# Unused bytes between the operand blocks of a matmul stream on one Trainium2 core

## The chip, the cores and the metric

The kernel runs on one core of one Trainium2 chip. The metric is the device time of one execution in microseconds (us); the lower the better. Three runs of the kernel before are given, and one execution of it was profiled. Engines are named as in the profile: PE is TensorE (matmuls), PEld its weight loads, DVE is VectorE, ACT is ScalarE, POOL is GpSimd and SP is SyncE, which issues the DMAs.

## The reference, cut to what matters

The input x is 16 sequences of 128 x 128. A mixture of experts with all eight experts evaluated densely, and a shared expert, are added to it, and then a 128 x 128 matrix picked for each sequence is applied and added.

```python
# x (16,128,128), gating (16,8), sg (16,1,1); Wg, Wu (8,128,512), Wd (8,512,128)
g = einsum('bsd,edf->ebsf', x, Wg);  u = einsum('bsd,edf->ebsf', x, Wu)
expert_outs = einsum('ebsf,efd->ebsd', silu(g) * u, Wd)
expert_output = einsum('be,ebsd->bsd', gating, expert_outs)
shared = einsum('bsf,fd->bsd', silu(x @ Sg) * (x @ Su), Sd)
x = x + (1 - sg) * expert_output + sg * shared
out = x + einsum('bij,bjk->bik', T[step - 1], x)
```

## The kernel before, in words

Everything is held transposed: features on the 128 partitions, and the 16 x 128 = 2048 tokens in the free dimension, in NT = 4 tiles of W = 512 columns. The hidden dimension of 512 is cut into NC = 4 chunks of 128. An expert is thus 16 units (4 tiles x 4 chunks), and with the shared expert there are 9 x 16 = 144 units.

To keep accuracy at the speed of the type fp32r, each fp32 operand is split into a high part (the value rounded to fp32r, `_hi`) and a low part (the rest, `_lo`), and each product is three matmuls: high x high, high x low and low x high. A unit n has three products and so nine matmuls of 512 columns, each with its own weight load of 128 columns:

- `project_g` (lines 444 to 446, into `g_bank`) multiplies gate weights by the x tile,
- `project_u` (the same lines, into `u_bank`) the up weights by the x tile,
- `project_down` (lines 470, 471 and 473, into `o_bank`) the down weights by the h tile of two units before (LAG = 2).

144 units are 1296 such matmuls. Between them ACT computes silu (L278), DVE multiplies (L342), ACT rounds h into `h_hi` (L284), DVE subtracts to get `h_lo` (L348). Every four units DVE scales the expert's output (L356) and POOL adds it to `acc` (L260).

The weights arrive by DMA in `w_raw`, which holds two experts (slots), four chunks and three matrices. For every expert POOL rounds each chunk of three blocks at once into `w_hi` (L217, 128 x 384) and subtracts for `w_lo` (L212); the first expert's are rounded by ACT (L297) and subtracted by DVE (L382) and POOL (L212), in other shapes. The x tiles are split once, in the beginning (L294, L307, L233, L385). The order of the PE work is the program's: no scheduler is involved. Semaphores guard each hand-over, and PE waits for a new expert's weights at the first unit of an expert.

Tiles lie in SBUF one behind the other in the order of their declaration. A weight block is 128 x 4 bytes = 512 bytes on each partition, an x tile or h tile 2048 bytes, and each tensor declared ahead of them has a multiple of 512 bytes.

The end of the program transposes the result (L483), multiplies by the picked matrices (L491) and stores.

Of the kernel before, what the change touches and what calls it, by code (L numbers as in the profile page):

```python
# [5 lines left out]
P = 128  # L6
# [6 lines left out]
def moe_then_step_kernel(  # L13
# [33 lines left out]
    W = BT * S  # L47
# [6 lines left out]
    PEEL_DVE = 5  # L54
    EARLY = 3
    Q = 32
    assert NC == 4 and NT == 4 and E % 2 == 0

    with ExitStack() as ctx:
# [6 lines left out]
        x_nat = sb("x_nat", [P, BT, D])  # L66
        x_blk = sb("x_blk", [P, B, S])
        zero = sb("zero", [P, P])
        x_hi = sb("x_hi", [P, NT, W], F32R)
        x_lo = sb("x_lo", [P, NT, W], F32R)  # L70
        w_raw = sb("w_raw", [P, 2, NC, 3, P])
        w_hi = sb("w_hi", [P, 2, NC, 3, P], F32R)
        w_lo = sb("w_lo", [P, 2, NC, 3, P], F32R)
        silu_g = sb("silu_g", [P, 2, W])
        h_hi = sb("h_hi", [P, HR, W], F32R)
        h_lo = sb("h_lo", [P, HR, W], F32R)
        scaled = sb("scaled", [P, 2, W])
        acc = sb("acc", [P, NT, W])
        yT = sb("yT", [P, NT, W])
# [123 lines left out]
        @block.gpsimd  # L203
        def _(pool):
            nc.gpsimd.memset(ident[:, :], 0.0).then_inc(ident_done, 1)
            pool.wait_ge(ident_done, 1)
            nc.gpsimd.affine_select(out=ident[:, :], in_=ident[:, :], compare_op=ALU.not_equal, fill=1.0, base=0,
                                    pattern=[[-1, P]], channel_multiplier=1).then_inc(ident_done, 1)

            def low_part(slot, c, m):  # L210

                return nc.gpsimd.tensor_tensor(w_lo[:, slot, c, m, :], w_raw[:, slot, c, m, :],  # L212
                                               w_hi[:, slot, c, m, :].bitcast(F32), ALU.subtract)

            def split_chunk(slot, c, count):

                nc.gpsimd.tensor_copy(w_hi[:, slot, c, :, :], w_raw[:, slot, c, :, :]).then_inc(w_rounded, 1)  # L217
                pool.wait_ge(w_rounded, count + 1)
                low_part(slot, c, slice(0, 3)).then_inc(w_ready, 1)


            pool.wait_ge(w0_rounded, 3)
            low_part(0, 1, slice(0, 2)).then_inc(w_ready, 1)
            pool.wait_ge(w0_rounded, 4)
            low_part(0, 2, slice(0, 2)).then_inc(w_ready, 1)
            low_part(0, 3, slice(0, 2)).then_inc(w_ready, 1)
            pool.wait_ge(w0_rounded, 5)
            low_part(0, slice(0, NC), 2).then_inc(w_ready, 1)

            def split_x(t):  # L230

                pool.wait_ge(x_rounded, t + 1)
                nc.gpsimd.tensor_tensor(x_lo[:, t, :], acc[:, t, :], x_hi[:, t, :].bitcast(F32),  # L233
                                        ALU.subtract).then_inc(acc_done, 1)

            split_x(1)

            pool.wait_ge(c_in, 32)
            nc.gpsimd.tensor_scalar(rest_b[:, :], share_b[:, :], -1.0, 1.0, ALU.mult, ALU.add).then_inc(coef_step, 1)
            nc.gpsimd.tensor_copy(coef[:, E * B:(E + 1) * B], share_b[:, :]).then_inc(coef_step, 1)  # L240
            pool.wait_ge(coef_step, 2)
            nc.gpsimd.tensor_tensor(coef[:, 0:E * B].rearrange("p (e b) -> p b e", b=B), route_b[:, :, :],
                                    rest_b[:, :].unsqueeze(2).to_broadcast([P, B, E]), ALU.mult).then_inc(coef_step, 1)
            for t in range(2, NT):
                split_x(t)

            with pool.Fori(0, E, 2) as e:
                for par in range(2):  # L250
                    slot = (par + 1) % 2
                    for t in range(NT):
                        group = NT * (e + par) + t
                        if t == 0:

                            pool.wait_ge(w_in[slot], 24 * e + 48)

                        pool.wait_ge(acc_done, group + NT - 1)
                        pool.wait_ge(scaled_done, group + 1)
                        nc.gpsimd.tensor_tensor(acc[:, t, :], acc[:, t, :], scaled[:, t % 2, :], ALU.add).then_inc(acc_done, 1)  # L260
                        if t < 2:
                            for c in (2 * t, 2 * t + 1):
                                split_chunk(slot, c, NC * (e + par) + c)


            for t in range(NT):
                tile = slice(t * BT, (t + 1) * BT)
                pool.wait_ge(T_turned, t + 1)
                nc.gpsimd.tensor_tensor(T_plus[:, tile, :], T_turn[:, tile, :],
                                        ident[:, :].unsqueeze(1).to_broadcast([P, BT, P]), ALU.add).then_inc(T_done, 1)  # L270

        @block.scalar
        def _(act):
# [6 lines left out]
            def round_h(n, k):  # L280


                act.wait_ge(h_done, n + 1)
                nc.scalar.activation(h_hi[:, k % HR, :], u_bank[k % HR][:, :], ACT.Copy).then_inc(h_rounded, 1)  # L284

            def copy_y(i):
                b, nb = parts[i]
# [3 lines left out]

            def round_x(t):
                act.wait_ge(x_turned, t)
                nc.scalar.activation(x_hi[:, t, :], acc[:, t, :], ACT.Copy).then_inc(x_rounded, 1)  # L294

            def round_w0(c, m):
                nc.scalar.activation(w_hi[:, 0, c, m, :], w_raw[:, 0, c, m, :], ACT.Copy).then_inc(w0_rounded, 1)  # L297


            act.wait_ge(zero_done, 1)  # L300
# [3 lines left out]
            act.wait_ge(wu0_in, 16)  # L304
            round_w0(0, 1)
            act.wait_ge(x0_turned, 1)
            nc.scalar.activation(x_hi[:, 0, :], o_bank[0][:, :], ACT.Copy).then_inc(x_rounded, 1)  # L307
            act.wait_ge(w0_in, 32)
            round_w0(1, slice(0, 2))
            round_w0(slice(2, NC), slice(0, 2))  # L310
# [26 lines left out]
        def _(dve):  # L337
# [7 lines left out]
            def split_h(n, k):  # L345

                dve.wait_ge(h_rounded, n + 1)
                nc.vector.tensor_tensor(h_lo[:, k % HR, :], u_bank[k % HR][:, :], h_hi[:, k % HR, :].bitcast(F32),  # L348
                                        ALU.subtract).then_inc(split_done, 1)

            def scale_group(m0, t):
# [27 lines left out]
            for m in range(2):  # L379

                dve.wait_ge(w0_rounded, m + 1)
                nc.vector.tensor_tensor(w_lo[:, 0, 0, m, :], w_raw[:, 0, 0, m, :], w_hi[:, 0, 0, m, :].bitcast(F32),  # L382
                                        ALU.subtract).then_inc(split_done, 1)
            dve.wait_ge(x_rounded, 1)
            nc.vector.tensor_tensor(x_lo[:, 0, :], o_bank[0][:, :], x_hi[:, 0, :].bitcast(F32),  # L385
                                    ALU.subtract).then_inc(split_done, 1)

            nc.vector.tensor_copy(acc[:, 0, :], o_bank[0][:, :])
# [52 lines left out]
        def _(pe):  # L441
            def product(bank, w, x_h, x_l, start, stop):

                nc.tensor.matmul(bank, w_hi[:, w[0], w[1], w[2], :], x_h, start=start, stop=False)  # L444
                nc.tensor.matmul(bank, w_hi[:, w[0], w[1], w[2], :], x_l, start=False, stop=False)  # L445
                return nc.tensor.matmul(bank, w_lo[:, w[0], w[1], w[2], :], x_h, start=False, stop=stop)  # L446

            def project_g(n, k):

                t, c = k % U // NC, k % NC  # L450

                pe.wait_ge(g_read, n - 1)
                product(g_bank[k % 2][:, :], (k // U % 2, c, 0), x_hi[:, t, :], x_lo[:, t, :],
                        True, True).then_inc(g_done, 1)

            def project_u(n, k):
                t, c = k % U // NC, k % NC
                if k >= LAG:

                    pe.wait_ge(split_done, EARLY + n + 1 - HR)  # L460
                product(u_bank[k % HR][:, :], (k // U % 2, c, 1), x_hi[:, t, :], x_lo[:, t, :],
                        True, True).then_inc(u_done, 1)

            def project_down(n, k):
# [2 lines left out]
                w = (k // U % 2, c, 2)  # L467

                pe.wait_ge(h_rounded, n + 1)
                nc.tensor.matmul(o_bank[t % 2][:, :], w_hi[:, w[0], w[1], w[2], :], h_hi[:, slot, :], start=c == 0, stop=False)  # L470
                nc.tensor.matmul(o_bank[t % 2][:, :], w_lo[:, w[0], w[1], w[2], :], h_hi[:, slot, :], start=False, stop=False)  # L471
                pe.wait_ge(split_done, EARLY + n + 1)
                last = nc.tensor.matmul(o_bank[t % 2][:, :], w_hi[:, w[0], w[1], w[2], :], h_lo[:, slot, :],  # L473
                                        start=False, stop=c == NC - 1)
                if c == NC - 1:
                    last.then_inc(o_done, 1)
# [30 lines left out]
            warm_up(2)  # L507

            pe.wait_ge(x_rounded, 1)
            nc.tensor.matmul(g_bank[0][:, :], w_hi[:, 0, 0, 0, :], x_hi[:, 0, :], start=True, stop=False)  # L510
            pe.wait_ge(split_done, 1)
            nc.tensor.matmul(g_bank[0][:, :], w_lo[:, 0, 0, 0, :], x_hi[:, 0, :], start=False, stop=False)
            pe.wait_ge(split_done, EARLY)
            nc.tensor.matmul(g_bank[0][:, :], w_hi[:, 0, 0, 0, :], x_lo[:, 0, :], start=False, stop=True).then_inc(g_done, 1)
            project_u(0, 0)

            pe.wait_ge(w_ready, 1)
            product(g_bank[1][:, :], (0, 1, 0), x_hi[:, 0, :], x_lo[:, 0, :], True, True).then_inc(g_done, 1)
            project_u(1, 1)
            with pe.Fori(0, N_ROUTED // U, 2) as e:  # L520
                for k in range(LAG, 2 * U + LAG):
# [56 lines left out]
```

## Time and profile before

| | |
|---|---|
| median of 3 runs | 312.31 us (312.09 to 312.71) |
| the profiled execution | 312.09 us |
| its span, first to last instruction | 310.1 us |
| busy shares of the span | PE 99%, PEld 82%, DVE 70%, ACT 53%, POOL 33% |
| share of PE in the chain that ended last | 95% |
| granted TensorE clock | full speed (2.4 GHz) in all slices |

A matmul's record is longer than the time to the start of the next one, since they are pipelined; the busy share of PE therefore says less than the distance between starts.

### The profile page before, as it was taken

To read this page: it belongs to the slowest core of one execution; us is meant where nothing else is said; L and a number is where in the kernel's file an instruction comes from. 1 tells how busy PE (TensorE), PEld (TensorE's weight loads), DVE (VectorE), ACT (ScalarE), POOL (GpSimd) and SP (SyncE) were. 2 spreads that over 40 slices of the span, in tenths; PEclk is the share of its full clock that TensorE was granted. 3 is DMA by queue.
4 is the path that set the end of the run, shared out by engine and by line. 5 is a ranking of instruction groups with operands and counts; after the bars stand their busy time and mean duration, and the time that the engine had idled before them with its cause. 6 is when DMAs were issued, how large, how long until landed. Compare 5 with 4: busy or idle time off the path is not lost.

```text
span 310.1 us, 4762 instructions
## 1 busy us (share of the span) xinstructions
PE 305.5 (99%) x1364; PEld 253.3 (82%) x1364; DVE 217.5 (70%) x355; ACT 164.6 (53%) x306; POOL 102.2 (33%) x116
## 2 busy tenths in 40 slices
PE   8999999999999999999999999999999999999996
PEld 7688888888888888888888888888888888888885
DVE  2786667766676666776667766677666766668885
ACT  5565555555555555555555555555555555555552
POOL 2565312441155115511552134411441155111310
PEclk9999999999999999999999999999999999999999
DMA  6930300030001100030003001100013000000112
GB/s 159 201 89 2 103 1 2 0 94 7 1 0 45 56 0 0 0 101 0 0 0 109 13 13 17 17 14 13 15 17 110 0 0 0 0 2 0 34 36 68
DMA packets 32727, 10.39 MB, mean 34 GB/s; under 512 B 16208, under 2 KB 32720, under 8 KB 32720
## 3 DMA queue, kind: packets, MB, share of 16 engines
q1 hardware_dynamic: 32720, 10.30, 13.5%
q8 instruction: 4, 0.07, 0.1%
q14 instruction: 3, 0.02, 0.0%
HBM read 9.25 MB, written 1.05 MB: 33 GB/s over the span
## 4 chain that ended last, share of the span: by engine, by line
PE 95%; SPq 1%; DMA 1%; POOL 0%; DVE 0%; ACT 0%; issue 0%
PE o_bank L470 11%; PE o_bank L473 11%; PE o_bank L471 11%; PE g_bank L446 10%; PE u_bank L446 10%; PE g_bank L445 10%; PE u_bank L445 10%; PE g_bank L444 10%; PE u_bank L444 10%; DMA w_raw<-in_L_cond_Wd 1%; PE o_bank L491 1%; SPq L158 1%; PE o_bank L483 0%; POOL w_lo L212 0%; DVE res L371 0%; PE u_bank L483 0%
## 5 line engine op out<-in xcount | busy, mean ns | idle before, releaser
L342 DVE TENSOR_TENSOR u_bank<-u_bank,silu_g 128x512 f32<-128x512 f32 x144 | 100.7, 699 | 84.2 <-PE u_bank L446 82.6
L278 ACT ACTIVATE silu_g<-g_bank 128x512 f32<-128x512 f32 x144 | 86.1, 598 | 132.8 <-PE g_bank L446 132.4
L348 DVE TENSOR_TENSOR h_lo<-u_bank,h_hi 128x512 fp32r<-128x512 f32 x144 | 97.9, 680 | 0.1
L260 POOL TENSOR_TENSOR acc<-acc,scaled 128x512 f32<-128x512 f32 x32 | 41.5, 1296 | 163.2 <-DVE scaled L356 163.0
L284 ACT ACTIVATE h_hi<-u_bank 128x512 fp32r<-128x512 f32 x144 | 85.4, 593 | 0.7 <-DVE u_bank L342 0.7
L470 PE MATMUL o_bank<-h_hi,w_hi 128*128 128x512 f32 x144 | 56.2, 390 | 0.8 <-POOL w_lo L212 0.8
L444 PE MATMUL u_bank<-x_hi,w_hi 128*128 128x512 f32 x144 | 56.1, 390 | 0.0
L473 PE MATMUL o_bank<-h_lo,w_hi 128*128 128x512 f32 x144 | 56.0, 389 | 0.0
L445 PE MATMUL u_bank<-x_lo,w_hi 128*128 128x512 f32 x144 | 56.0, 389 | 0.0
L471 PE MATMUL o_bank<-h_hi,w_lo 128*128 128x512 f32 x144 | 56.0, 389 | 0.0
L446 PE MATMUL u_bank<-x_hi,w_lo 128*128 128x512 f32 x144 | 56.0, 389 | 0.0
L444 PE MATMUL g_bank<-x_hi,w_hi 128*128 128x512 f32 x143 | 56.0, 392 | 0.0
L445 PE MATMUL g_bank<-x_lo,w_hi 128*128 128x512 f32 x143 | 55.7, 389 | 0.0
L446 PE MATMUL g_bank<-x_hi,w_lo 128*128 128x512 f32 x143 | 55.6, 389 | 0.0
L212 POOL TENSOR_TENSOR w_lo<-w_raw,w_hi 128x384 fp32r<-128x384 f32 (+2 forms) x36 | 35.8, 998 | 9.1 <-ACT w_hi L297 6.5
L470 PEld LDWEIGHTS o_bank<-h_hi,w_hi 128*128 128x128 f32 x144 | 27.0, 188 | 6.7 <-POOL w_lo L212 1.2
L445 PEld LDWEIGHTS u_bank<-x_lo,w_hi 128*128 128x128 f32 x144 | 27.1, 188 | 5.7
L444 PEld LDWEIGHTS u_bank<-x_hi,w_hi 128*128 128x128 f32 x144 | 27.2, 189 | 5.6
L473 PEld LDWEIGHTS o_bank<-h_lo,w_hi 128*128 128x128 f32 x144 | 27.0, 188 | 5.7 <-DVE h_lo L348 0.2
L471 PEld LDWEIGHTS o_bank<-h_hi,w_lo 128*128 128x128 f32 x144 | 27.0, 188 | 5.6
L446 PEld LDWEIGHTS u_bank<-x_hi,w_lo 128*128 128x128 f32 x144 | 27.0, 188 | 5.6
L446 PEld LDWEIGHTS g_bank<-x_hi,w_lo 128*128 128x128 f32 x143 | 26.8, 188 | 5.5
(49 smaller groups left out, 151.2 us busy)
## 6 DMA issues: line engine op xcount, KB each, us to landing
w_raw<-in_L_cond_Wd SPq DMA_DIRECT2D x8, 256.0 KB, 3.9
w_raw<-in_L_cond_Wg SPq DMA_DIRECT2D x7, 256.0 KB, 3.1
w_raw<-in_L_cond_Wu SPq DMA_DIRECT2D x7, 256.0 KB, 3.8
T_blk<-in_L_cond_T SPq DMA_DIRECT2D x64, 16.0 KB, 1.6
out_y<-res SPq DMA_DIRECT2D x3, 256.0 KB, 2.3
x_blk<-in_x SPq DMA_DIRECT2D x4, 128.0 KB, 3.6
x_nat<-in_x SPq DMA_DIRECT2D x1, 256.0 KB, 2.8
x_blk<-in_x SPq DMA_DIRECT2D x4, 64.0 KB, 2.7
```

Source lines behind the costliest of these rows:

```text
L212: return nc.gpsimd.tensor_tensor(w_lo[:, slot, c, m, :], w_raw[:, slot, c, m, :], w_hi[:, slot, c, m, :].bitcast(F32), ALU.subtract)
L260: nc.gpsimd.tensor_tensor(acc[:, t, :], acc[:, t, :], scaled[:, t % 2, :], ALU.add).then_inc(acc_done, 1)
L278: nc.scalar.activation(silu_g[:, k % 2, :], g_bank[k % 2][:, :], ACT.Silu).then_inc(g_read, 1)
L284: nc.scalar.activation(h_hi[:, k % HR, :], u_bank[k % HR][:, :], ACT.Copy).then_inc(h_rounded, 1)
L342: nc.vector.tensor_tensor(u_bank[k % HR][:, :], u_bank[k % HR][:, :], silu_g[:, k % 2, :], ALU.mult).then_inc(h_done, 1)
L348: nc.vector.tensor_tensor(h_lo[:, k % HR, :], u_bank[k % HR][:, :], h_hi[:, k % HR, :].bitcast(F32), ALU.subtract).then_inc(split_done, 1)
L444: nc.tensor.matmul(bank, w_hi[:, w[0], w[1], w[2], :], x_h, start=start, stop=False)
L445: nc.tensor.matmul(bank, w_hi[:, w[0], w[1], w[2], :], x_l, start=False, stop=False)
L446: return nc.tensor.matmul(bank, w_lo[:, w[0], w[1], w[2], :], x_h, start=False, stop=stop)
L470: nc.tensor.matmul(o_bank[t % 2][:, :], w_hi[:, w[0], w[1], w[2], :], h_hi[:, slot, :], start=c == 0, stop=False)
L471: nc.tensor.matmul(o_bank[t % 2][:, :], w_lo[:, w[0], w[1], w[2], :], h_hi[:, slot, :], start=False, stop=False)
L473: last = nc.tensor.matmul(o_bank[t % 2][:, :], w_hi[:, w[0], w[1], w[2], :], h_lo[:, slot, :], start=False, stop=c == NC - 1)
```

## The change

The tensors get unused columns of 4 bytes: each weight block in `w_hi` and `w_lo` is followed by 4 (16 bytes, so blocks are 528 bytes apart and no longer 512), each x tile in `x_hi` and `x_lo` by 16 (64 bytes, 2112 in place of 2048), and each h tile in `h_hi` and `h_lo` by 8 (32 bytes, 2080 in place of 2048). All accesses name the used columns. `w_raw`, `acc` and all others keep their shapes, but lie elsewhere, as the tensors ahead of them have grown. No instruction is added, removed or moved. Wherever an instruction writes or reads several blocks of `w_hi` or `w_lo` at once, its access is no longer one run but one run for each block.

```diff
+    WP = P + 4
+    XP = W + 16
+    HP = W + 8
...
-        x_hi = sb("x_hi", [P, NT, W], F32R)
-        x_lo = sb("x_lo", [P, NT, W], F32R)
+        x_hi = sb("x_hi", [P, NT, XP], F32R)
+        x_lo = sb("x_lo", [P, NT, XP], F32R)
         w_raw = sb("w_raw", [P, 2, NC, 3, P])
-        w_hi = sb("w_hi", [P, 2, NC, 3, P], F32R)
-        w_lo = sb("w_lo", [P, 2, NC, 3, P], F32R)
+        w_hi = sb("w_hi", [P, 2, NC, 3, WP], F32R)
+        w_lo = sb("w_lo", [P, 2, NC, 3, WP], F32R)
         silu_g = sb("silu_g", [P, 2, W])
-        h_hi = sb("h_hi", [P, HR, W], F32R)
-        h_lo = sb("h_lo", [P, HR, W], F32R)
+        h_hi = sb("h_hi", [P, HR, HP], F32R)
+        h_lo = sb("h_lo", [P, HR, HP], F32R)
...
-                nc.gpsimd.tensor_copy(w_hi[:, slot, c, :, :], w_raw[:, slot, c, :, :]).then_inc(w_rounded, 1)
+                nc.gpsimd.tensor_copy(w_hi[:, slot, c, :, 0:P], w_raw[:, slot, c, :, :]).then_inc(w_rounded, 1)
...
-                nc.scalar.activation(h_hi[:, k % HR, :], u_bank[k % HR][:, :], ACT.Copy).then_inc(h_rounded, 1)
+                nc.scalar.activation(h_hi[:, k % HR, 0:W], u_bank[k % HR][:, :], ACT.Copy).then_inc(h_rounded, 1)
...
-                nc.tensor.matmul(bank, w_hi[:, w[0], w[1], w[2], :], x_h, start=start, stop=False)
-                nc.tensor.matmul(bank, w_hi[:, w[0], w[1], w[2], :], x_l, start=False, stop=False)
-                return nc.tensor.matmul(bank, w_lo[:, w[0], w[1], w[2], :], x_h, start=False, stop=stop)
+                nc.tensor.matmul(bank, w_hi[:, w[0], w[1], w[2], 0:P], x_h, start=start, stop=False)
+                nc.tensor.matmul(bank, w_hi[:, w[0], w[1], w[2], 0:P], x_l, start=False, stop=False)
+                return nc.tensor.matmul(bank, w_lo[:, w[0], w[1], w[2], 0:P], x_h, start=False, stop=stop)
```

The other changed lines put `0:P` or `0:W` in place of `:` in the same way.

## Rows read from the trace of the kernel before

**Rows 1.** The page's chain that ended last, by engine.

```profile
PE 95%; SPq 1%; DMA 1%; POOL 0%; DVE 0%; ACT 0%; issue 0%
```

**Rows 2.** The chain in order of time: start us, us, what.

```profile
11.45 0.50 PE o_bank L470
...
302.86 0.44 PE o_bank L483 x4
...
304.69 0.89 PE o_bank L491 x8
305.58 0.66 PE u_bank L483 x4
```

**Rows 3.** Waits of PE: engine line, waited for, us, times, longest.

```profile
PE o_bank L470 <- POOL w_lo L212: 0.8, 1, 0.8
```

**Rows 4.** Timeline of one unit: start us, us, engine, line, operation.

```profile
102.05 0.39 PE L444 MATMUL g_bank<-x_hi,w_hi 128*128 128x512 f32 x1
102.05 0.19 PEld L445 LDWEIGHTS g_bank<-x_lo,w_hi 128*128 128x128 f32 x1
...
102.27 0.39 PE L445 MATMUL g_bank<-x_lo,w_hi 128*128 128x512 f32 x1
...
102.73 0.39 PE L444 MATMUL u_bank<-x_hi,w_hi 128*128 128x512 f32 x1
...
103.41 0.39 PE L470 MATMUL o_bank<-h_hi,w_hi 128*128 128x512 f32 x1
...
104.09 0.39 PE L444 MATMUL g_bank<-x_hi,w_hi 128*128 128x512 f32 x1
```

**Rows 5.** PE in windows as long as an expert: busy us (records), clock, DMA.

```profile
20.00:52.64 32.64, 32.64 (x146) 1.00 0.09 26
...
150.56:183.20 32.64, 32.64 (x146) 1.00 0.13 32
...
248.48:281.12 32.64, 32.64 (x146) 1.00 0.00 1
```

**Rows 6.** Tile w_hi: duration ns min/median/max, first and last start us.

```profile
L444 PE MATMUL u_bank<-x_hi,w_hi x144: 389/389/465, 7.0 to 300.7; 128*128 128x512 f32 x144
...
L470 PEld LDWEIGHTS o_bank<-h_hi,w_hi x144: 186/188/190, 11.4 to 303.6; 128*128 128x128 f32 x144
L470 PE MATMUL o_bank<-h_hi,w_hi x144: 389/389/497, 11.4 to 303.8; 128*128 128x512 f32 x144
```

**Rows 7.** Timeline: the unit after the first wait for weights.

```profile
12.02 0.39 PE L473 MATMUL o_bank<-h_lo,w_hi 128*128 128x512 f32 x1
...
14.10 0.39 PE L473 MATMUL o_bank<-h_lo,w_hi 128*128 128x512 f32 x1
```

**Rows 8.** POOL's groups by form: busy us, mean ns, idle before.

```profile
L212 POOL TENSOR_TENSOR w_lo<-w_raw,w_hi 128x384 fp32r<-128x384 f32 x32 | 32.4, 1014 | 2.6
L217 POOL CAST w_hi<-w_raw 128x384 fp32r<-128x384 f32 x32 | 16.2, 507 | 0.0
...
L212 POOL TENSOR_TENSOR w_lo<-w_raw,w_hi 128x256 fp32r<-128x256 f32 x3 | 2.1, 736 | 5.1 <-ACT w_hi L297 5.1
L212 POOL TENSOR_TENSOR w_lo<-w_raw,w_hi 128x512 fp32r<-128x512 f32 x1 | 1.3, 1277 | 1.4 <-ACT w_hi L297 1.4
```

**Rows 9.** POOL's timeline around the weights of one expert.

```profile
93.47 1.29 POOL L260 TENSOR_TENSOR acc<-acc,scaled 128x512 f32<-128x512 f32 x1 [3.85 <-DVE scaled L356]
...
96.84 1.02 POOL L212 TENSOR_TENSOR w_lo<-w_raw,w_hi 128x384 fp32r<-128x384 f32 x1
101.63 1.29 POOL L260 TENSOR_TENSOR acc<-acc,scaled 128x512 f32<-128x512 f32 x1 [3.77 <-DVE scaled L356]
```

**Rows 10.** ACT's groups by form.

```profile
L284 ACT ACTIVATE h_hi<-u_bank 128x512 fp32r<-128x512 f32 x144 | 85.4, 593 | 0.7 <-DVE u_bank L342 0.7
...
L297 ACT ACTIVATE w_hi<-w_raw 128x512 fp32r<-128x512 f32 x2 | 1.2, 624 | 1.5 <-DMA w_raw<-in_L_cond_Wd 1.5
```

More of the change, by code:

```diff
@@ L210, in low_part @@
             def low_part(slot, c, m):
-                return nc.gpsimd.tensor_tensor(w_lo[:, slot, c, m, :], w_raw[:, slot, c, m, :],
-                                               w_hi[:, slot, c, m, :].bitcast(F32), ALU.subtract)
+                return nc.gpsimd.tensor_tensor(w_lo[:, slot, c, m, 0:P], w_raw[:, slot, c, m, :],
+                                               w_hi[:, slot, c, m, 0:P].bitcast(F32), ALU.subtract)
             def split_chunk(slot, c, count):
-                nc.gpsimd.tensor_copy(w_hi[:, slot, c, :, :], w_raw[:, slot, c, :, :]).then_inc(w_rounded, 1)
+                nc.gpsimd.tensor_copy(w_hi[:, slot, c, :, 0:P], w_raw[:, slot, c, :, :]).then_inc(w_rounded, 1)
                 pool.wait_ge(w_rounded, count + 1)
@@ L232, in split_x @@
                 pool.wait_ge(x_rounded, t + 1)
-                nc.gpsimd.tensor_tensor(x_lo[:, t, :], acc[:, t, :], x_hi[:, t, :].bitcast(F32),
+                nc.gpsimd.tensor_tensor(x_lo[:, t, 0:W], acc[:, t, :], x_hi[:, t, 0:W].bitcast(F32),
                                         ALU.subtract).then_inc(acc_done, 1)
@@ L293, in round_x @@
                 act.wait_ge(x_turned, t)
-                nc.scalar.activation(x_hi[:, t, :], acc[:, t, :], ACT.Copy).then_inc(x_rounded, 1)
+                nc.scalar.activation(x_hi[:, t, 0:W], acc[:, t, :], ACT.Copy).then_inc(x_rounded, 1)
             def round_w0(c, m):
-                nc.scalar.activation(w_hi[:, 0, c, m, :], w_raw[:, 0, c, m, :], ACT.Copy).then_inc(w0_rounded, 1)
+                nc.scalar.activation(w_hi[:, 0, c, m, 0:P], w_raw[:, 0, c, m, :], ACT.Copy).then_inc(w0_rounded, 1)
             act.wait_ge(zero_done, 1)
@@ L306, in _ @@
             act.wait_ge(x0_turned, 1)
-            nc.scalar.activation(x_hi[:, 0, :], o_bank[0][:, :], ACT.Copy).then_inc(x_rounded, 1)
+            nc.scalar.activation(x_hi[:, 0, 0:W], o_bank[0][:, :], ACT.Copy).then_inc(x_rounded, 1)
             act.wait_ge(w0_in, 32)
@@ L347, in split_h @@
                 dve.wait_ge(h_rounded, n + 1)
-                nc.vector.tensor_tensor(h_lo[:, k % HR, :], u_bank[k % HR][:, :], h_hi[:, k % HR, :].bitcast(F32),
+                nc.vector.tensor_tensor(h_lo[:, k % HR, 0:W], u_bank[k % HR][:, :], h_hi[:, k % HR, 0:W].bitcast(F32),
                                         ALU.subtract).then_inc(split_done, 1)
@@ L381, in _ @@
                 dve.wait_ge(w0_rounded, m + 1)
-                nc.vector.tensor_tensor(w_lo[:, 0, 0, m, :], w_raw[:, 0, 0, m, :], w_hi[:, 0, 0, m, :].bitcast(F32),
+                nc.vector.tensor_tensor(w_lo[:, 0, 0, m, 0:P], w_raw[:, 0, 0, m, :], w_hi[:, 0, 0, m, 0:P].bitcast(F32),
                                         ALU.subtract).then_inc(split_done, 1)
             dve.wait_ge(x_rounded, 1)
-            nc.vector.tensor_tensor(x_lo[:, 0, :], o_bank[0][:, :], x_hi[:, 0, :].bitcast(F32),
+            nc.vector.tensor_tensor(x_lo[:, 0, 0:W], o_bank[0][:, :], x_hi[:, 0, 0:W].bitcast(F32),
                                     ALU.subtract).then_inc(split_done, 1)
@@ L452, in project_g @@
                 pe.wait_ge(g_read, n - 1)
-                product(g_bank[k % 2][:, :], (k // U % 2, c, 0), x_hi[:, t, :], x_lo[:, t, :],
+                product(g_bank[k % 2][:, :], (k // U % 2, c, 0), x_hi[:, t, 0:W], x_lo[:, t, 0:W],
                         True, True).then_inc(g_done, 1)
@@ L460, in project_u @@
                     pe.wait_ge(split_done, EARLY + n + 1 - HR)
-                product(u_bank[k % HR][:, :], (k // U % 2, c, 1), x_hi[:, t, :], x_lo[:, t, :],
+                product(u_bank[k % HR][:, :], (k // U % 2, c, 1), x_hi[:, t, 0:W], x_lo[:, t, 0:W],
                         True, True).then_inc(u_done, 1)
@@ L469, in project_down @@
                 pe.wait_ge(h_rounded, n + 1)
-                nc.tensor.matmul(o_bank[t % 2][:, :], w_hi[:, w[0], w[1], w[2], :], h_hi[:, slot, :], start=c == 0, stop=False)
-                nc.tensor.matmul(o_bank[t % 2][:, :], w_lo[:, w[0], w[1], w[2], :], h_hi[:, slot, :], start=False, stop=False)
+                nc.tensor.matmul(o_bank[t % 2][:, :], w_hi[:, w[0], w[1], w[2], 0:P], h_hi[:, slot, 0:W], start=c == 0, stop=False)
+                nc.tensor.matmul(o_bank[t % 2][:, :], w_lo[:, w[0], w[1], w[2], 0:P], h_hi[:, slot, 0:W], start=False, stop=False)
                 pe.wait_ge(split_done, EARLY + n + 1)
-                last = nc.tensor.matmul(o_bank[t % 2][:, :], w_hi[:, w[0], w[1], w[2], :], h_lo[:, slot, :],
+                last = nc.tensor.matmul(o_bank[t % 2][:, :], w_hi[:, w[0], w[1], w[2], 0:P], h_lo[:, slot, 0:W],
                                         start=False, stop=c == NC - 1)
@@ L509, in _ @@
             pe.wait_ge(x_rounded, 1)
-            nc.tensor.matmul(g_bank[0][:, :], w_hi[:, 0, 0, 0, :], x_hi[:, 0, :], start=True, stop=False)
+            nc.tensor.matmul(g_bank[0][:, :], w_hi[:, 0, 0, 0, 0:P], x_hi[:, 0, 0:W], start=True, stop=False)
             pe.wait_ge(split_done, 1)
-            nc.tensor.matmul(g_bank[0][:, :], w_lo[:, 0, 0, 0, :], x_hi[:, 0, :], start=False, stop=False)
+            nc.tensor.matmul(g_bank[0][:, :], w_lo[:, 0, 0, 0, 0:P], x_hi[:, 0, 0:W], start=False, stop=False)
             pe.wait_ge(split_done, EARLY)
-            nc.tensor.matmul(g_bank[0][:, :], w_hi[:, 0, 0, 0, :], x_lo[:, 0, :], start=False, stop=True).then_inc(g_done, 1)
+            nc.tensor.matmul(g_bank[0][:, :], w_hi[:, 0, 0, 0, 0:P], x_lo[:, 0, 0:W], start=False, stop=True).then_inc(g_done, 1)
             project_u(0, 0)
             pe.wait_ge(w_ready, 1)
-            product(g_bank[1][:, :], (0, 1, 0), x_hi[:, 0, :], x_lo[:, 0, :], True, True).then_inc(g_done, 1)
+            product(g_bank[1][:, :], (0, 1, 0), x_hi[:, 0, 0:W], x_lo[:, 0, 0:W], True, True).then_inc(g_done, 1)
             project_u(1, 1)
```

## The prediction

> **What bounds the kernel now.** I read the page's chain first: 95% of the span lies on PE [rows 1]. The chain in order of time shows where PE's stream begins and ends: it starts in earnest at 11.45 us and hands over to the tail of small transposes and matmuls at 305.58 us [rows 2]. The view of PE's waits has one wait of this stream, 0.8 us for the first expert's low weights at 11.45 us [rows 3]; after it PE waits for nobody. So the time is a number of matmuls by the distance between their starts, and the third view is the timeline of one unit. From the start of its first matmul at 102.05 us to that of the next unit's at 104.09 us pass 2.04 us for nine matmuls, 226.7 ns each [rows 4]. The windows of an expert's length confirm it to the last digit: a stretch of 32.64 us holds 16 units, and each of them has the same 146 records (144 matmuls and the two cut by its edges) at full clock [rows 5]; there are eight such windows from 20 to 281 us, of which three stand there.
>
> The sum: before 11.45 us PE has done the g and u products of units 0, 1 and 2, 18 matmuls. The other 1278 by 226.7 ns are 289.7 us. Three transposes of 0.44 us and three steps of 0.89 us between them are 4.0 us [rows 2]. From 305.58 us to the end of the span are 4.5 us. 11.45 + 289.7 + 4.0 + 4.5 = 309.7 us, against a span of 310.1 us; the 0.4 us left are units a little slower right after an interruption, as the one from 12.02 to 14.10 us, 2.08 us in place of 2.04 [rows 7]. The profiled execution took 312.09 us, 2.0 us more than its span, and lies 0.2 us under the median of 312.31 us.
>
> At 2.4 GHz, 226.7 ns are 544 cycles for 512 columns. 32 cycles (13.3 ns) are thus not columns, 17.3 us over 1296 matmuls, and whether the change reaches them is the whole question.
>
> **The change part by part.**
>
> *PE's two reads.* While the 512 columns of one matmul are read, the weights of the next are loaded: the load of L445 starts at 102.05 us with the matmul of L444, and its record is 0.19 us long [rows 4]. Do these two reads hinder each other by where they lie? Before, all weight blocks begin at multiples of 512 bytes and all tiles too, so the pairs differ in their distance, but never in the distance modulo 512 bytes. What the trace excludes: a hindrance that depends on the address above 512 bytes. A window of an expert's length runs through 4 x tiles, 4 h slots and 12 blocks of high and of low weights, the windows alternate between both weight slots, and the pairs lie from next to each other to tens of kilobytes apart. Yet g, u and down products are alike spaced [rows 4], all windows hold the same count [rows 5], and weight loads vary only from 186 to 190 ns over 144 records [rows 6]. What the trace can't exclude is a hindrance by the low nine bits of the address, since those are now the same for all.
>
> Two things speak against this as well. First, the two reads go at different paces: the load's 128 columns of 4 bytes in at most 188 ns and the matmul's 512 in some 213 ns, so while the load reads its 512 bytes the matmul reads some 1.8 KB, and the one passes the other's place modulo 512 more than twice. A constant offset of 16 to 500 bytes between the starts shifts when they meet, not how often. Second, other readers and writers of SBUF come and go (DMA at a share of 0.13 and of 0.00 [rows 5], POOL reading and writing weights at one time and idle at another [rows 9]) at any address, and the 226.7 ns don't move. I take 0 ns per matmul. Bounds: the most that can be won is all of the 13.3 ns, 17.3 us; the most that can be lost, by the nearest row in which the stream went slower (2.08 us a unit, 4.4 ns per matmul [rows 7]), is 5.8 us. The value is near neither end: no row shows a dependence on address at all. The smallest step of a synchronous stream, one cycle of 0.42 ns in each matmul, would be 0.54 us.
>
> A rule of the Trainium skill speaks against a gain here: the page "TensorE: Matmul & The Clock Gate", section "Step-by-step: what each phase is for", says that the engine has two independent SBUF read ports, one for the moving operand and one for the weight load, which takes no bandwidth from the running matmul. By it the sum stays at 312.3 us; the trace agrees as far as the spacing doesn't vary with the pair, and can't show what the spacing would be without a load.
>
> *POOL's splits.* The cast L217 writes three runs of 128 in place of one of 384, and L212 reads and writes such. It may cost nothing: L212 took 1277 ns in the form of 4 blocks that already lie apart (the third matrix of all chunks) and 1014 and 736 ns in the joined forms of 3 and 2 blocks; the steps are 278 and 263 ns per block, so lying apart shows no cost [rows 8]. If both got a third dearer, a pair of chunks would take 4.1 us in place of 3.0 us. Its cover: after L212 at 96.84 us POOL idles 3.8 us until the next sum at 101.63 us [rows 9], and the weights split there by 97.86 us are needed only at the next expert's first unit, which is the one at 104.09 us [rows 4] (the sum at 101.63 us is that of the third tile, which DVE scales just ahead of the fifteenth unit): 6.2 us of slack. Without that cover each expert would pay 2 us. I take 0.
>
> *ACT and DVE.* `h_hi` and `h_lo` are still one run of 512 each; ACT's 593 ns [rows 10] and DVE's have no cause to change, and PE doesn't wait for either [rows 3]. The first expert's rounding by ACT is on the path: the wait of 0.8 us at 11.45 us hangs behind L297 of the down weights and L212 of 1277 ns. Both already step over blocks (every third one), so only the step changes, from 1536 to 1584 bytes. 0 us; at worst L212 pays the rate of its dearest form (736 ns for 256, or 2.88 ns for each element, against 2.49), 0.2 us, and ACT the difference of 624 to 593 ns, 0.03 us [rows 8, 10].
>
> *Everything else.* Tensors behind lie at other addresses, still multiples of 128 bytes as the padded sizes add up; DMAs have the same pieces and PE waits for none. 0 us.
>
> Sum: 0 us on the profiled execution's 312.09 us, and on the median: 312.3 us.
>
> **The rivals.**
>
> *A: the 32 cycles are a conflict of equal low addresses, and spreading them dissolves it.* For it: 32 is also the number of 16-byte pieces in a weight block's row of 512 bytes, and today every pair has the same phase. Against it: the differing paces. All gone gives 312.3 - 17.3 = 295.0 us; half of it, if the new phases still meet in half of the pairs, 303.7 us. The same page of the Trainium skill (section "Back-to-back issue gap") gives N / 2.4 + 2.5 ns between warm matmuls. By that rule 10.8 ns of the spacing here would be avoidable and the time an estimated 298.3 us; no run here shows 215.8 ns.
>
> *B, the other side: blocks that start off a round address are read more slowly.* Today all start at multiples of 512 bytes. After it, of the 24 weight blocks of a tensor no two would begin at the same place modulo 512, half begin off 32 bytes, and every second h tile off 64 bytes. A weight load has cover: 188 ns in a spacing of 226.7 ns, so it must grow by more than 38 ns to be seen. A moving read has none, each ns shows. If the odd h slots alone pay the 4.4 ns of the slow unit [rows 7], 216 matmuls make 1.0 us: 313.3 us. If all pay, 5.8 us: 318.1 us. It decides from 0.5 ns a matmul on average. The same price holds where equal phases are free of conflict today and the new ones are not.
>
> *C: POOL gets so slow with broken runs that weights come late.* A pair of chunks takes 3.0 us and has 6.2 us until PE needs it [rows 4, 9]; it would have to triple. I give it no price but a place in "slower".
>
> **How the numbers follow.** Differences within 0.2% (0.6 us) can't be told from none; the three runs before span that much. No effect: 0.80. Rival A: 0.09, all of it faster. Rival B and C: 0.11, slower. The forecast is that of the likeliest, 312.3 us. The range takes one cycle a matmul either way (0.54 us), the spread of the runs (0.2 below, 0.4 above) and the 0.2 us of the start above: 311.5 to 313.4, and leaves out rival A and the dear half of B. That is some 15 in 100.
>
> **What the profile of the changed kernel would show.** Right: units of 2.04 us, the same 146 records in 32.64 us, loads of 188 ns, matmul records of 389 ns, L217 near 507 and L212 near 1014 ns, the first wait near 0.8 us. Rival A: fewer than 2.04 us a unit, and units that differ from each other, as the pairs now differ in phase. Rival B: moving reads of h (L470, L471, L473) spaced wider than those of x, in every second unit. C: PE waits for w_lo of L212 beyond the first. The prediction is wrong if the spacing depends on the low bits of an address, which no pair of the kernel before could show.

## The result, and the profile after

The changed kernel takes 317.91 us (median of 3 runs, 317.58 to 317.91) against 312.31 us: a ratio of 1.0174, with an interval of 1.0151 to 1.0197. It is 5.6 us slower, where 312.3 us was forecast with a range up to 313.4 us. The profiled execution has a span of 315.8 us, 5.7 us more than before.

The page's chain by engine reads as before [rows 1]: PE holds the end, and nobody else has moved into the chain.

```profile
PE 95%; SPq 1%; DMA 1%; POOL 0%; DVE 0%; ACT 0%; issue 0%
```

The chain in order of time (start us, us, what) answers to [rows 2]. PE's stream of down products begins 0.55 us earlier, since the first down weights happened to land sooner, and it ends 5.66 us later. All of the loss, and 0.55 us more, lies within the stream.

```profile
10.90 0.49 PE o_bank L473
...
308.53 0.44 PE o_bank L486 x4
310.35 0.89 PE o_bank L494 x8
311.24 0.66 PE u_bank L486 x4
```

PE's waits have no new row (L473 is L470 of before, the lines are three further down); the one that answers to [rows 3] is a little shorter:

```profile
PE o_bank L473 <- POOL w_lo L215: 0.6, 1, 0.6
```

The same windows of an expert's length as in [rows 5] (busy us, records, clock, DMA share, GB/s) hold 142 or 143 records and no longer 146, at the same clock:

```profile
20.00:52.64 32.64, 32.64 (x142) 1.00 0.09 26
...
85.28:117.92 32.64, 32.64 (x143) 1.00 0.08 24
```

So the matmuls are further apart, all along the stream. One window of 260 us, from 20 to 280 us, measures it: before it held 1149 records, after 1124. Less the two that the edges cut, the mean distance between starts was 260 / 1147 = 226.7 ns and is 260 / 1122 = 231.7 ns. Over the 1278 matmuls of the stream these 5.0 ns are 6.4 us; less the 0.55 us of earlier start that is 5.8 us, against the 5.7 us by which the span grew.

```profile
20.00:280.00 260.00, 260.00 (x1124) 1.00 0.09 22
```

The timeline of PE shows two things that answer to [rows 4]: a unit now takes 2.08 us (101.33 to 103.41), and the steps within it are no longer alike, some 0.22 or 0.23 us and some 0.24 us.

```profile
101.33 0.39 PE L447 MATMUL g_bank<-x_hi,w_hi 128*128 128x512 f32 x1
101.56 0.40 PE L448 MATMUL g_bank<-x_lo,w_hi 128*128 128x512 f32 x1
101.80 0.39 PE L449 MATMUL g_bank<-x_hi,w_lo 128*128 128x512 f32 x1
102.03 0.39 PE L447 MATMUL u_bank<-x_hi,w_hi 128*128 128x512 f32 x1
102.25 0.39 PE L448 MATMUL u_bank<-x_lo,w_hi 128*128 128x512 f32 x1
102.48 0.39 PE L449 MATMUL u_bank<-x_hi,w_lo 128*128 128x512 f32 x1
102.71 0.39 PE L473 MATMUL o_bank<-h_hi,w_hi 128*128 128x512 f32 x1
102.94 0.40 PE L474 MATMUL o_bank<-h_hi,w_lo 128*128 128x512 f32 x1
103.18 0.39 PE L476 MATMUL o_bank<-h_lo,w_hi 128*128 128x512 f32 x1
103.41 0.39 PE L447 MATMUL g_bank<-x_hi,w_hi 128*128 128x512 f32 x1
```

The pattern belongs to the pairs and not to chance: two experts (66.7 us) later, at the same blocks and tiles, the same steps come back, 0.24 us behind L448 among them.

```profile
168.05 0.39 PE L447 MATMUL g_bank<-x_hi,w_hi 128*128 128x512 f32 x1
168.28 0.40 PE L448 MATMUL g_bank<-x_lo,w_hi 128*128 128x512 f32 x1
168.52 0.39 PE L449 MATMUL g_bank<-x_hi,w_lo 128*128 128x512 f32 x1
```

The records of the single instructions say little on where it lies: in the view of tile w_hi (duration ns min/median/max, first and last start us; compare [rows 6]) the weight load still takes 188 ns, while the matmul's record grew from 389 to 394 ns. A matmul's end is modelled, so its 5 ns are a hint only, and that the load's record stays as it was holds for this kernel and not for all (see w_shift below).

```profile
L473 PEld LDWEIGHTS o_bank<-h_hi,w_hi x144: 186/188/190, 10.9 to 309.3; 128*128 128x128 f32 x144
L473 PE MATMUL o_bank<-h_hi,w_hi x144: 387/394/494, 10.9 to 309.5; 128*128 128x512 f32 x144
```

And POOL's groups by form cost what they did [rows 8], broken runs or not:

```profile
L215 POOL TENSOR_TENSOR w_lo<-w_raw,w_hi 128x384 fp32r<-128x384 f32 x32 | 32.6, 1019 | 2.6
L220 POOL CAST w_hi<-w_raw 128x384 fp32r<-128x384 f32 x32 | 16.2, 507 | 0.0
```

### The profile page after: what moved, and what is told of

It is laid out like the page before. It is cut to its first block, busy times and chain, and to the rows that moved or that the text cites. A ratio compares the mean times of both kernels' runs of the same rounds, so it can differ in the third digit from the quotient of the medians.

```text
span 315.8 us, 4762 instructions
## 1 busy us (share of the span) xinstructions
PE 311.3 (99%) x1364; PEld 252.8 (80%) x1364; DVE 217.8 (69%) x355; ACT 164.8 (52%) x306; POOL 102.4 (32%) x116
## 4 chain that ended last, share of the span: by engine, by line
PE 95%; SPq 1%; DMA 1%; POOL 0%; DVE 0%; ACT 0%; issue 0%
PE o_bank L473 11%; PE o_bank L474 11%; PE o_bank L476 11%; PE u_bank L447 10%; PE u_bank L449 10%; PE u_bank L448 10%; PE g_bank L447 10%; PE g_bank L448 10%; PE g_bank L449 10%; DMA w_raw<-in_L_cond_Wd 1%; PE o_bank L494 1%; SPq L161 1%; PE o_bank L486 0%; POOL w_lo L215 0%; DVE res L374 0%; PE u_bank L486 0%
## 5 line engine op out<-in xcount | busy, mean ns | idle before, releaser
L473 PE MATMUL o_bank<-h_hi,w_hi 128*128 128x512 f32 x144 | 57.0, 396 | 0.6 <-POOL w_lo L215 0.6
L474 PE MATMUL o_bank<-h_hi,w_lo 128*128 128x512 f32 x144 | 56.8, 394 | 0.0
L449 PE MATMUL u_bank<-x_hi,w_lo 128*128 128x512 f32 x144 | 56.7, 394 | 0.0
L476 PE MATMUL o_bank<-h_lo,w_hi 128*128 128x512 f32 x144 | 56.7, 394 | 0.0
L448 PE MATMUL u_bank<-x_lo,w_hi 128*128 128x512 f32 x144 | 56.7, 394 | 0.0
L448 PE MATMUL g_bank<-x_lo,w_hi 128*128 128x512 f32 x143 | 56.2, 393 | 0.0
L473 PEld LDWEIGHTS o_bank<-h_hi,w_hi 128*128 128x128 f32 x144 | 27.0, 188 | 7.2 <-POOL w_lo L215 1.0
L448 PEld LDWEIGHTS u_bank<-x_lo,w_hi 128*128 128x128 f32 x144 | 27.0, 188 | 6.2
L447 PEld LDWEIGHTS g_bank<-x_hi,w_hi 128*128 128x128 f32 x143 | 26.9, 188 | 6.2 <-POOL w_lo L215 0.2
```

The lines of the kernel that those rows point to most:

```text
L447: nc.tensor.matmul(bank, w_hi[:, w[0], w[1], w[2], 0:P], x_h, start=start, stop=False)
L448: nc.tensor.matmul(bank, w_hi[:, w[0], w[1], w[2], 0:P], x_l, start=False, stop=False)
L449: return nc.tensor.matmul(bank, w_lo[:, w[0], w[1], w[2], 0:P], x_h, start=False, stop=stop)
```

## The experiments

Each kernel ran beside the kernel before on the same chip; its ratio is against that. The kernel before took 311.5 to 311.8 us there. The spacing is the mean distance between starts, worked out as above from the records in the window from 20 to 280 us of the one execution that was profiled; the time and the ratio are of all executions.

Where blocks and tiles lie: all starts of the kernel before are equal modulo 512 bytes. They are not multiples of 512, as the text ahead of the result has it, but lie 128 bytes past one; only their differences are multiples. "Distance" below is the start of the weight blocks less the start of the tiles, modulo 256, and is 0 for it.

**One pad at a time.** The edits set two of the three pads back to nothing:

```diff
-    WP, XP, HP = P + 4, W + 16, W + 8    # the change
+    WP, XP, HP = P + 4, W, W             # w_pads
+    WP, XP, HP = P, W + 16, W            # x_pads
+    WP, XP, HP = P, W, W + 8             # h_pads
```

Expected, of w_pads, x_pads and h_pads in this order:

> Only the weight blocks are padded (528 bytes apart), the x and h tiles lie as before. Theory 1, the distance modulo 512 bytes between the weight block being loaded and the tile being read sets the cost, so that any spread of the phases costs the whole amount: about 317.5 to 318 us, 231.5 ns per matmul on average, for x and h products alike. Theory 2, the start of the weight block off a multiple of 32 or 64 bytes costs: the same 317.5 to 318 us. Theory 3, the start of the moving tile costs: 312.3 us, 226.7 ns.

> Only the x tiles are padded (2112 bytes apart). Theory 1 (distance modulo 512): the distance is 64, 128 or 192 bytes off today's for three of four tiles and 256 off for the low part, so the 864 gate and up matmuls pay for most of their pairs and the 432 down matmuls pay nothing: 312.3 + about 700 x 4.9 ns = 315.7 us. Theory 2 (start of the weight block): 312.3 us. Theory 3 (start of the moving tile): 312.3 us where 64 bytes are round enough, otherwise as theory 1.

> Only the h tiles are padded (2080 bytes apart). Theory 1 (distance modulo 512): three of four h slots are off today's distance, so about 324 of the 432 down matmuls pay 4.9 ns, 313.9 us, and the gate and up matmuls keep 226.7 ns. Theory 2: 312.3 us. Theory 3: 313.4 to 313.9 us.

Measured: w_pads 318.24 us (ratio 1.0204, interval 1.0187 to 1.0221), 231.7 ns; x_pads 316.88 us (1.017, 1.0153 to 1.0187), 230.7 ns; h_pads 315.02 us (1.01, 1.0083 to 1.0117), 229.3 ns; the window held 1124, 1129 and 1136 records. Each pad costs by itself, the weights' at least as much as all three. Theories 2 and 3 fall as the only cause, since the x and h pads cost with all weight blocks on starts equal modulo 512 as before, and the weights' pads cost with all tiles so. The pads don't add up (6.5, 5.1 and 3.2 us against 5.6 us together), as one has to expect if what counts is whether a pair is off, and not by how many pads. The theory's numbers miss: x_pads and h_pads were to cost 3.4 and 1.6 us. In part it is the count and the price that were off. By the addresses 648 pairs of x_pads are off, and 360 of h_pads in place of the 324 expected, since the padding moves the whole tensor `h_lo` by 128 bytes. At the 6.7 ns that a wrong distance of 16 or 32 bytes costs below, these would be 4.3 and 2.4 us. The rest falls on matmuls whose own pairs are at 0: in x_pads these are 229.1 ns from the next on average, not 226.7, and in h_pads the x products, all at 0, are 227.7 ns. The timeline of x_pads shows how:

```profile
79.37 0.39 PE L473 MATMUL o_bank<-h_hi,w_hi 128*128 128x512 f32 x1
79.60 0.39 PE L474 MATMUL o_bank<-h_hi,w_lo 128*128 128x512 f32 x1
79.83 0.39 PE L476 MATMUL o_bank<-h_lo,w_hi 128*128 128x512 f32 x1
80.05 0.40 PE L447 MATMUL g_bank<-x_hi,w_hi 128*128 128x512 f32 x1
...
83.54 0.40 PE L473 MATMUL o_bank<-h_hi,w_hi 128*128 128x512 f32 x1
83.78 0.39 PE L474 MATMUL o_bank<-h_hi,w_lo 128*128 128x512 f32 x1
84.01 0.39 PE L476 MATMUL o_bank<-h_lo,w_hi 128*128 128x512 f32 x1
84.24 0.40 PE L447 MATMUL g_bank<-x_hi,w_hi 128*128 128x512 f32 x1
```

At 79.37 us the first x tile is in use, whose distances are 0 here too, and three down products take 0.68 us. At 83.54 us it is the next tile, 64 bytes off, and the three down products take 0.70 us, though their own distances are still 0. In all units of the window whose x tile is the first the three take 0.680 us, in all whose x tile is the second 0.697 or 0.698 us. A matmul's loss thus reaches over to its neighbours.

**The same distance for all pairs.** With no pads, only the place of the weights was moved (and for `all_shift` that of x, h and weights together), by asking for a longer run and using it from an offset:

```diff
-        w_hi = sb("w_hi", [P, 2, NC, 3, P], F32R)
+        w_hi = sb("w_hi", [P, 2 * NC * 3 * P + 128], F32R)[:, 4:4 + 2 * NC * 3 * P].rearrange(
+            "p (a b c d) -> p a b c d", a=2, b=NC, c=3, d=P)     # 4 columns = 16 bytes
```

The offset was 4 in w_shift, 8, 16, 32 and 64 in w_shift32, 64, 128 and 256, and 124, 120 and 96 in w_back16, 32 and 128; the all_shift kernels do it for all six tensors, xh_shift16 for those of x and h alone.

Expected, of w_shift, w_shift32, w_shift64, w_shift128, w_back128, w_shift256, w_back16 and w_back32 in this order:

> No pads between blocks, but all weight blocks of both tensors begin 16 bytes later, so that every pair of block and tile has the same distance modulo 512, 16 bytes more than before. Theory 1: all 1296 matmuls are spaced alike again, at a value other than 226.7 ns if a distance of 16 bytes matters (about 231 ns, 318 us), and at 226.7 ns if that distance is one of the free ones. Theory 2 (a block that begins off 32 bytes costs): all spaced alike and wider, by about twice 4.9 ns if only the half of the blocks that lie off 32 bytes paid in the changed kernel: 318 to 325 us. Theory 4, only a variety of phases costs, as when the reads fall into step with each other in a uniform stream: 312.3 us.

> Weight blocks alone begin 32 bytes later; every pair has the distance 32 modulo 512. Distance theory: one uniform spacing again, above 226.7 ns unless 32 is a free distance; I expect 230 to 236 ns and 316 to 323 us. Start theory (off 32 bytes costs): back at 312 us, since the blocks begin at a multiple of 32 bytes again.

> Weight blocks alone begin 64 bytes later, starts on multiples of 32, distance 64 for all. If every distance off a multiple of 256 costs: 231 to 233.5 ns, 318 to 320.5 us. If the period were 64: 311.8 us; but 128 bytes already cost 5.7 ns, so that would be odd.

> Weight blocks alone begin 128 bytes later. In the kernel with padded x tiles the pairs at 128 or 384 bytes modulo 512 had mixed spacings and those at 256 kept 226.7 ns. Distance theory with a period of 256 bytes: a cost, 229 to 234 ns, 315 to 321 us. Distance theory with a period of 128 or less: 312 us. Start theory: 312 us.

> Weight blocks begin 384 bytes later: 128 bytes short of the old phase, which is also 128 ahead if the period is 256. Period 256: the same as 128 bytes ahead, 232.4 ns, 318.8 us. Period 512: another value, as behind is cheaper than ahead: 226.7 to 229 ns.

> Weight blocks alone begin 256 bytes later. In the kernel with padded x tiles the pairs at a distance of 256 bytes modulo 512 kept 226.7 ns. Distance theory with a period of 256 bytes: 311.5 us, 226.7 ns everywhere. Period of 512: 229 to 234 ns, 315 to 321 us.

> Weight blocks alone begin 496 bytes later, 16 bytes short of the old phase. If only the size of the distance counts, the same as 16 bytes ahead: 233.3 ns, 320.3 us. If the order counts (which of the two reads comes to a place first, since they run at different paces), another value; it may even lie under 226.7 ns, and then a version faster than the kernel before exists.

> Weight blocks begin 480 bytes later, 32 bytes short of the old phase, on a multiple of 32. 16 bytes short cost 1.7 ns, 16 ahead 6.7, 32 ahead 6.7. If a distance behind is cheap as such: 226.7 to 229 ns, 311.5 to 314.5 us. If the cost grows with the distance either way: 233 ns, 320 us.

| kernel | distance | us | ratio (interval) | spacing |
|---|---|---|---|---|
| w_shift | +16 | 320.29 | 1.0276 (1.0259 to 1.0293) | 233.4 ns |
| w_shift32 | +32 | 319.96 | 1.0275 (1.0257 to 1.0292) | 233.4 ns |
| w_shift64 | +64 | 319.94 | 1.0264 (1.0246 to 1.0283) | 233.6 ns |
| w_shift128 | +128 | 318.76 | 1.0246 (1.0224 to 1.0267) | 232.6 ns |
| w_back128 | -128 | 318.78 | 1.0222 (1.0205 to 1.0239) | 232.6 ns |
| w_back32 | -32 | 320.26 | 1.0264 (1.0242 to 1.0285) | 233.4 ns |
| w_back16 | -16 | 313.52 | 1.0056 (1.0037 to 1.0075) | 228.3 ns |
| w_shift256 | 256 = 0 | 311.89 | 0.9996 (0.9986 to 1.0006) | 226.7 ns |

Four windows, of w_shift, w_back16, w_shift128 and w_shift256 in this order, with the counts from which the spacings come:

```profile
20.00:280.00 260.00, 260.00 (x1116) 1.00 0.09 22
```

```profile
20.00:280.00 260.00, 260.00 (x1141) 1.00 0.09 22
```

```profile
20.00:280.00 260.00, 260.00 (x1120) 1.00 0.09 22
```

```profile
20.00:280.00 260.00, 260.00 (x1149) 1.00 0.09 22
```

What follows: no variety is needed, one wrong distance for all costs more (7 to 8.5 us) than the change's mixture, except 16 bytes behind (2.1 us). The period is 256 bytes: 256 is free, and 128 ahead and 128 behind have the same spacing (and 7.3 and 7.0 us over the kernel before on their chips). The idea that a distance behind is cheap as such was wrong (32 behind costs all of it), and so was the hope for a distance better than 0. Why 16 bytes behind costs only 1.7 ns, I can't say. A distance of 16 either way always has a start off 32 bytes in it, so these two rows don't show the distance alone; the other six do.

"Uniform" is the distance and not the step. In w_shift the steps are 230 to 236 ns, but in w_shift128, where the distance is the same for all pairs, they go from 228 to 241 ns and come back every seven matmuls, while the program's unit is nine long. At 10 ns the timeline shows it in the matmuls' records, three of 0.40 us and four of 0.39 us:

```profile
101.39 0.40 PE L476 MATMUL o_bank<-h_lo,w_hi 128*128 128x512 f32 x1
101.62 0.40 PE L447 MATMUL g_bank<-x_hi,w_hi 128*128 128x512 f32 x1
101.86 0.40 PE L448 MATMUL g_bank<-x_lo,w_hi 128*128 128x512 f32 x1
102.09 0.39 PE L449 MATMUL g_bank<-x_hi,w_lo 128*128 128x512 f32 x1
102.32 0.39 PE L447 MATMUL u_bank<-x_hi,w_hi 128*128 128x512 f32 x1
102.56 0.39 PE L448 MATMUL u_bank<-x_lo,w_hi 128*128 128x512 f32 x1
102.78 0.39 PE L449 MATMUL u_bank<-x_hi,w_lo 128*128 128x512 f32 x1
103.01 0.40 PE L473 MATMUL o_bank<-h_hi,w_hi 128*128 128x512 f32 x1
103.25 0.40 PE L474 MATMUL o_bank<-h_hi,w_lo 128*128 128x512 f32 x1
103.49 0.40 PE L476 MATMUL o_bank<-h_lo,w_hi 128*128 128x512 f32 x1
```

In the trace's single nanoseconds a step of 240 or 241 ns stands at every seventh matmul of the window, 160 of them. So a matmul's step depends on its own pair and on what the matmuls before it left behind, and a price for each pair can only be a mean.

The load's record isn't always untouched either. In w_shift it is 192 ns in the middle, not 188, for some of the products:

```profile
L448 PEld LDWEIGHTS u_bank<-x_lo,w_hi x144: 187/192/193, 6.9 to 308.1; 128*128 128x128 f32 x144
```

**Everything moved together.** Expected, of all_shift16, all_shift32, all_shift64 and all_shift128 in this order:

> Weight blocks, x tiles and h tiles all begin 16 bytes later, without pads between them: the starts are off 32 bytes as in the kernel that shifted the weights alone, the distance of each pair is a multiple of 512 bytes as in the kernel before. Theory 1 (distance): the time of before, 311.8 to 312.3 us, and 226.7 ns per matmul. Theory 2 or 3 (start of block or tile off 32 bytes): about 320 us, 233.3 ns, as with the weights alone shifted.

> Blocks and tiles all begin 32 bytes later, distances stay multiples of 512. With 16 bytes the profiled run was spaced 233.3 ns. If the start of a tile off a multiple of 32 bytes costs: 311.5 us here, 226.7 ns. If off a multiple of 64 bytes costs: 316 to 320 us. If the distance alone counted, 16 bytes would have been free as well, so that theory has to be widened by the start of the tile in any case.

> The same with 64 bytes. Start off a multiple of 64 costs: 311.5 us, 226.7 ns here. Start off 128 costs: 316 to 320 us. If any move of the tiles costs, even with equal distances, what counts is their place against something else that stayed (the raw weights, or nothing in the program): 316 to 320 us here too.

> The same with 128 bytes; in the kernel before all starts are at 128 modulo 512 (the first tensor begins there). Start off 128 is what costs, or less: 311.5 us. A rule of 256 bytes for the start: 316 to 320 us.

Measured: by 32 bytes 311.65 us (ratio 1.0001, 0.9988 to 1.0014), by 64 bytes 312.08 us (1.0002, 0.999 to 1.0015), by 128 bytes 311.91 us (0.9999, 0.9988 to 1.001), with 1149, 1149 and 1148 records in the window, 226.7 to 226.9 ns. In steps of 32 bytes the absolute place doesn't count; only the relation of weights to tiles does. These kernels also moved the six tensors against the raw weights and the sums, which ACT, DVE and POOL use, so the place of those isn't what counts. Nor does it count in w_shift whether another engine works: the 30 matmuls that start from 272.96 to 279.73 us, while POOL stands still, are spaced 233.4 ns as all are, and the steps taken while ACT or DVE works differ from those taken while it is idle by less than 0.1 ns on average. By 16 bytes, however, 317.52 us (1.0184, 1.016 to 1.0208) at distance 0. Its executions differ among themselves more than any other kernel's, 316.26, 317.45, 317.59 and, the profiled one, 319.70 us (those of w_back16, which also has a start off 32 bytes, come next with 311.86 to 313.89 us); the profiled one, the slowest of the four, was spaced 233.4 ns:

```profile
20.00:280.00 260.00, 260.00 (x1116) 1.00 0.09 22
```

The distance alone would give the time of before here, and that is wrong: there is a second condition.

**Which of the two must start on 32 bytes?**

> x and h tiles begin 16 bytes later, weight blocks as before: the distance is 16 bytes behind, as where the weights were moved by 496 bytes (228.3 ns, 313.5 us), but now the tile is off 32 bytes and the block is not. If distance alone counted: 228.3 ns, 313.5 us. If the tile's start off 32 bytes is what cost in the common shift by 16: about 233 ns, 318 to 320 us.

xh_shift16 has the distance of w_back16, 16 bytes behind, but the tile and not the block is off a multiple of 32. It took 317.71 us (1.0193, 1.0176 to 1.021) and 231.7 ns, against 313.52 us and 228.3 ns. So a tile that starts off 32 bytes costs; both kernels that have it show that (this one and all_shift16). For a weight block off 32 bytes there is w_back16, where it costs at most 1.7 ns. The window of xh_shift16:

```profile
20.00:280.00 260.00, 260.00 (x1124) 1.00 0.09 22
```

**Pads of other sizes.** All three pads stay, in other sizes:

```diff
-    WP, XP, HP = P + 4, W + 16, W + 8      # the change
+    WP, XP, HP = P + 64, W + 64, W + 64    # pads_256
+    WP, XP, HP = P + 8, W + 16, W + 8      # pads_32
```

Expected, of pads_256 and pads_32:

> All three pads as in the change, but each of 256 bytes, so that blocks are 768, x and h tiles 2304 bytes apart and every distance is a multiple of 256 bytes. If only the distance modulo 256 and the start modulo 32 count: 311.8 us, 226.7 ns. If blocks with gaps between them cost as such (on POOL, in reads of other lengths): about 317.5 us, as the change.

> The change with weight pads of 32 bytes in place of 16 (blocks 544 bytes apart), x and h pads as in the change: distances still vary in steps of 32, but every block and tile starts on a multiple of 32. If the varied distance is what costs: about 317.5 us, 231.5 ns, as the change. If the starts off 32 bytes carried it: 311.8 to 313.5 us.

pads_256 took 311.78 us (1.0003, 0.9992 to 1.0014), no different from the kernel before. Its window answers to [rows 5] with the same count:

```profile
20.00:52.64 32.64, 32.64 (x146) 1.00 0.09 26
```

pads_32, with every start on a multiple of 32 and varied distances, took 317.83 us (1.0192, 1.0175 to 1.021) and 231.9 ns, as much as the change with its blocks off 32:

```profile
20.00:280.00 260.00, 260.00 (x1123) 1.00 0.09 22
```

So it is neither gaps nor alignment to 16 or 32 bytes; the varied distances make up the whole cost of the change, within what the runs can tell.

## Why the prediction was wrong

**Right:** the bound and its sum. PE's stream alone sets the time, and the loss is its 1278 matmuls times a change of spacing. POOL's splits (1019 and 507 ns), ACT, DVE, the start and the DMAs cost nothing, as was taken. Rival C didn't occur.

**The step that failed** is in "PE's two reads": "A constant offset of 16 to 500 bytes between the starts shifts when they meet, not how often", and with it "I take 0 ns per matmul". The trace showed one phase only and the text said that the low bits couldn't be excluded; the argument from the two paces was put in the place of a row. The runs show the opposite: distance 0 modulo 256 costs nothing over the 226.7 ns, and every other one tried costs 5.9 to 6.9 ns where all pairs have it, but for 16 bytes behind. The term put at 0 ns measured 5.0 ns a matmul in the changed kernel, 6.4 us over the stream. "No row shows a dependence on address at all" was true and worth nothing, since no two pairs of the kernel differed in that respect. The second argument, that POOL and the DMAs come and go without effect, still holds and says nothing about a weight block and its tile.

**The upper bound was the value.** The loss bounded from the unit of 2.08 us [rows 7], 5.8 us, came out as 5.6 us. That is agreement by chance: that unit ran slower at a distance of 0, so it has another cause. It was a bound with a price, given too small a chance.

**Rival A** (equal phases are the conflict) is refuted with the sign turned: equal phases are the best case found. Of the rule of the Trainium skill that backed it (page "TensorE: Matmul & The Clock Gate", section "Back-to-back issue gap"), no run shows the 215.8 ns, which the page gives for a matmul by itself; none came under 226.7 ns on average.

**Rival B** had the side, and its last sentence the mechanism: "The same price holds where equal phases are free of conflict today and the new ones are not." Its main form, starts off a round address, is shown as a cost for tiles off 32 bytes alone (xh_shift16), and the change has none of these: its tiles are padded by 64 and 32 bytes. pads_32 shows that it has no share here. The sign in the profile that B was to give, h products slower in every second unit, isn't there; x and h products are both slower (231.4 and 232.1 ns on average), in every unit.

The other rule cited, that the engine reads moving operand and weights through two independent ports (same page, section "Step-by-step: what each phase is for"), doesn't cover this: moving the weights alone by 16 bytes cost 2.8%, and moving all by 32 cost nothing. The measurements decide.

**Open.** By which mechanism the distance acts wasn't shown: that the load for the next matmul collides with the reading of the current one is a guess that no run tested. The runs show only that the relation of the addresses counts, and a collision that concerned one pair alone would give neither the rhythm of seven matmuls nor the neighbours' loss. Whether the 13.3 ns over 512 columns that stay at distance 0 are of the same kind is open as well; no kernel had a matmul without a weight load beside it.

## What to carry to other kernels

In a stream of fp32r matmuls of 512 columns with a weight load for each, keep the starts of weight blocks and moving tiles equal modulo 256 bytes, and the tiles on multiples of 32: 512 byte blocks and 2048 byte tiles laid one behind the other do that by themselves, and a small tensor in between, or a pad for another purpose, can undo it for 0.6 to 2.8%. If a pad is needed, make it a multiple of 256 bytes. And where all pairs of a kernel share a property, its uniform trace says nothing about that property: bound it from both sides and give both real chances.

## What the runs showed of the hardware that was not expected

- The spacing of matmuls of 512 fp32r columns depends on the distance of weight block and tile modulo 256 bytes: 226.7 ns at 0, 228.3 ns at 16 bytes behind, 232.6 ns at 128, 233.4 to 233.6 ns at 16, 32 and 64 ahead and at 32 behind. These are means: at 128 the steps run from 228 to 241 ns in a rhythm of seven matmuls.
- A common shift off 32 bytes costs at distance 0 too (233.4 ns in the profiled execution), and the four executions of that program differ by up to 3.4 us.
- The cost shows in the matmul's record (389 to 394 ns) and hardly in the weight load's (188 ns, in w_shift 192 ns for some products), and neighbours with a good distance share it: 0.70 us in place of 0.68 us for three down products in x_pads.
